# A mixture-of-experts decoder layer: slots as a list of 8-byte pairs, rows gathered by GpSimd, routing and experts in one block

## What is computed

```python
y   = attn @ Wo + bo + x1                  # x1: output of the mixer
x2  = layernorm(y)
logits = x2 @ Wr + br                      # 8 experts
top2   = top_k(logits, 2);  w = softmax(of the two)
out = layernorm(x2 + sum_i w_i * (relu(x2 @ W1[e_i] + b1[e_i]) @ W2[e_i] + b2[e_i]))
```

## Time and profile before

| | us |
|---|---|
| median of three runs | 2315.91 (2313.05 to 2318.25) |
| the profiled execution | 2310.07 |
| its span, first to last instruction | 2308.3 |
| mixer and attention, until the routing block's first instruction | 1592.4 |
| routing block until the experts' first matmul | 165.5 |
| 71 expert tiles | 514.5 |
| final norm and stores | 34 |

### The profile page before, as it was taken

One profiled execution on the slowest core, in us unless ns is written; L12 is line 12 of the kernel. 1 busy time (PEld: TensorE's weight loads), 2 busy tenths in 40 slices (PEclk: granted clock), 3 DMA queues, 4 the chain that ended last, 5 costly groups with the idle time before them and its releaser, 6 DMA issues. The chain is left out here.

```text
span 2308.3 us, 41136 instructions
## 1 busy us (share of the span) xinstructions
PE 2011.2 (87%) x10638; PEld 1052.4 (46%) x10638; DVE 1736.3 (75%) x2834; ACT 1548.3 (67%) x4346; POOL 706.3 (31%) x919
## 2 busy tenths in 40 slices
PE   6988988499999999999999998886645999999993
PEld 2454555223222232222322221112545999999993
DVE  3978784399999999999999998985663555555554
ACT  3555565399999999999999999995211333333334
POOL 0001110044444344443444341111672333333331
PEclk9989999699999999999999999998767999999997
DMA  4111104646667576675765755644732222222224
GB/s 148 41 41 69 55 32 140 126 98 100 124 117 121 127 108 119 112 124 129 108 117 113 123 112 73 88 54 140 254 141 65 37 37 37 37 37 37 37 37 155
DMA packets 130110, 217.29 MB, mean 94 GB/s; under 512 B 20290, under 2 KB 100802, under 8 KB 129938
## 3 DMA queue, kind: packets, MB, share of 16 engines
q1 hardware_dynamic: 103072, 152.25, 35.6%
q0 software_dynamic: 25440, 63.46, 9.9%
q10 hardware_dynamic: 1554, 1.05, 0.2%
HBM read 137.97 MB, written 78.72 MB: 94 GB/s over the span
## 5 line engine op out<-in xcount | busy, mean ns | idle before, releaser
L1349 ACT ACTIVATE probs<-psum,neg_max 128x512 f32<-128x512 f32 (+1 forms) x1664 | 1110.8, 773 | 64.6 <-DVE neg_max L1257 63.1
L1257 DVE TENSOR_REDUCE neg_max<-psum 128x2 f32<-128x1024 f32 (+1 forms) x832 | 986.2, 1215 | 67.7 <-PE psum L1194 59.6
L1194 PE MATMUL psum<-qst,kst 96*128 96x512 bf16 (+1 forms) x1664 | 542.1, 394 | 111.6 <-ACT probs L1349 73.7
L1349 ACT ACTIVATION_READ_ACCUMULATOR probs<-psum,neg_max 128x1 f32 (+1 forms) x1664 | 488.7, 294 | 0.0
L1194 PEld LDWEIGHTS psum<-qst,kst 96*128 96x128 bf16 (+1 forms) x1664 | 130.5, 98 | 716.7 <-ACT probs L1349 655.3
L1162 PE MATMUL psum<-probs,v_scaled 128*32 128x512 f32 (+1 forms) x3328 | 454.6, 620 | 0.0
L1845 ACT ACTIVATE hid<-psum,b 128x128 f32<-128x128 f32 x568 | 162.0, 368 | 392.6 <-PE psum L1818 392.6
L1321 POOL TENSOR_TENSOR v_scaled<-vst,inv 128x64 f32<-128x64 f32 (+1 forms) x416 | 120.9, 291 | 707.0 <-DVE inv L1226 704.8
L1879 POOL DMA_INDIRECT sums_all<-y_out,dest x71 | 154.3, 2173 | 380.3 <-DVE y_out L1924 374.5
L1818 PE MATMUL psum<-xst,w 128*128 128x128 f32 x2272 | 266.6, 276 | 0.0
L1818 PEld LDWEIGHTS psum<-xst,w 128*128 128x128 f32 x2272 | 260.7, 193 | 0.1
(11 more groups left out here) (222 smaller groups left out, 2092.7 us busy)
## 6 DMA issues: line engine op xcount, KB each, us to landing
kst<-k_parts SPq DMA_DIRECT2D x384, 112.0 KB, 6.5
k_parts<-k_out POOLq DMA_DIRECT2D x52, 336.0 KB, 3.0
w_all<-in_W SPq DMA_DIRECT2D x16, 1024.0 KB
ct<-in_ctxT SPq DMA_DIRECT2D x16, 896.0 KB, 4.7
vst<-v_all SPq DMA_DIRECT2D x64, 224.0 KB, 9.2
qst<-q_parts SPq DMA_DIRECT2D x192, 64.0 KB, 5.9
v_all<-v_out POOLq DMA_DIRECT2D x13, 896.0 KB, 4.3
rows_in<-xs SPq DMA_DIRECT2D x71, 129.0 KB, 2.0
```

Source lines behind the costliest of these rows:

```text
L1194: last = pe.matmul(psum[0:r, 2 * sbuf + i, :], kst[:, h, j, t * P:t * P + r], qst[:, h, j, :], start=True, stop=True)
L1257: v.tensor_reduce(neg_max[0:r, sbuf], psum[0:r, 2 * sbuf:2 * sbuf + 2], AX_X, ALU.min) \
L1349: act.activation(probs[0:r, pb, j, :], psum[0:r, 2 * sbuf + i, :], ACT.Exp, bias=neg_max[0:r, sbuf, i:i + 1], scale=-1.0, accum_out=sums[0 ...
```

## The change

The rows of `x2` are no longer written to the slots. `list_all` holds for each slot 8 bytes: the token number and the weight. Pads are in it from the start: one DMA copies `no_pairs` (271 KB) over the whole list in the attention block, and another zeroes 128 pad rows of `x2_rows`. In the routing, `x2` is stored twice by SP, to `sums_all` and to `x2_rows`, and GpSimd writes 64 indirect DMAs of 128 pairs to the list. In the experts, SP loads 128 pairs of a tile three tiles ahead (`load_list`), VectorE casts the token numbers to `dest` (`name_rows`), and GpSimd gathers the rows of `x2_rows` with an indirect DMA two tiles ahead (`gather`). There are no pads to write at the end.

Routing and experts stand in one block. The routing is written out for 8 sequences instead of looped, and is three deep: in step c the sequence c is normed, c - 1 gets its experts, c - 2 its slots. The normed rows are now written by ScalarE (with a bias and a scale) instead of VectorE, and GpSimd's `residual` is replaced by a third matmul with one row of ones. The first two sequences' attention output and `x1`, `xwo` and W2 of expert 0 are loaded in the attention block. Buffers of the mixer and of the attention lie in the places of `w2_all` and of one shared `area`; W2 is laid out by the host as the chip holds it.

```diff
@@ attention block, SP
                     load_context(FIRST_UNITS)
+                    sp.dma_start(list_all, a["no_pairs"]).then_inc(list_cleared, 16)
+                    sp.dma_start(x2_rows[TOKENS:TOKENS + P], a["no_rows"]).then_inc(list_cleared, 16)
+                    for e in range(W2_EARLY):
+                        load_w2(sp, e)
...
                     for b in range(B - 2, B):
                         two_rounds(b, False)
                         load_weights(b)
+                        if b == B - 2:
+                            for h in range(2):
+                                sp.wait_ge(attn_stored[h], 16 * GH * 2 * (B - 1) + OPEN)
+                                load_route(sp, h)
+                            sp.dma_start(xwo, a["xWo"].rearrange("(c p) d -> p c d", p=P)).then_inc(xwo_loaded, 16)
@@ routing and experts, SP
+                    def route_step(c):
+                        h = c % 2
+                        if c < B and c + 2 < B:
+                            sp.wait_ge(y2_ready, c + 1)
+                            load_route(sp, c + 2)
+                        if c < B:
+                            sp.wait_ge(x2_ready, c + 1)
+                            for rows_to in (sums_all, x2_rows):
+                                sp.dma_start(rows_to[c * L:(c + 1) * L]..., x2[:, h]).then_inc(x2_stored[h], 16)
+                        for e in W2_IN_STEP.get(c, ()):      # {3: (1,), 4: (2,), 5: (3,), 6: (4, 5), 7: (6, 7)}
+                            load_w2(sp, e)
-                        sp.dma_start(rows_in[:, h], xs[bass.ds(row, P)]).then_inc(rows_loaded[h], 16)
+                        sp.dma_start(list_in[:, d], list_all[bass.ds(row, P)]).then_inc(list_loaded[d], 16)
+                    def tile_step(n, it, d, left):
+                        if left >= 3:
+                            sp.wait_ge(y_scaled, n + 1 + OPEN)
+                            load_list(bass.ds(n + 3, 1), (d + 3) % DESTS)
+                    sp.wait_ge(plan, ROWS_PLANNED)
+                    sp.wait_ge(scattered, 16 * 2 * TT * B)
+                    for j in range(3):
+                        load_list(slice(j, j + 1), j)
@@ GpSimd
+                    def scatter(e):
+                        pool.wait_ge(slots_ready, e + 1)
+                        for i in range(2):
+                            for t in range(TT):
+                                at = i * TT + t
+                                pool.indirect_dma_start(
+                                    list_all, bass.IndirectOffsetOnAxis(slot_u[:, e, at:at + 1], 0),
+                                    pairs[:, e, i, t, :], None).then_inc(scattered, 16)
+                    def gather(count, d):
+                        wait_alone(pool, (dest_ready, count))
+                        pool.indirect_dma_start(rows_in[:, d % 2], None, x2_rows,
+                                                bass.IndirectOffsetOnAxis(dest[:, d, :], 0)) \
+                            .then_inc(rows_loaded[d % 2], 16)
+                    def tile_step(n, it, d, left):
+                        h = d % 2
+                        if left >= 2:
+                            wait_alone(pool, (xs_t_ready, n + 1))
+                            gather(n + 3, (d + 2) % DESTS)
                         wait_alone(pool, (y_scaled, n + 2 + OPEN), (y_added[1 - h], ...))
                         pool.indirect_dma_start(sums_all, ..., y_out[:, h], None, compute_op=ALU.add)
@@ TensorE
+                            last = pe.matmul(at, ones[0:1, :], rows[0:1, XBO, :], start=False, stop=True)
+                    def route_step(c):
+                        if 0 <= c - 2 < B:
+                            ranks(c - 2)
+                        if 0 <= c - 1 < B:
+                            turn(c - 1)
+                        if c + 1 < B:
+                            project(c + 1, (0, 1))
+                        if 0 <= c - 1 < B:
+                            route(c - 1)
+                        if c + 1 < B:
+                            project(c + 1, (2, 3))
@@ VectorE
+                    def route_step(c):
+                        if c < B:
+                            norm_rows(c)
+                        if 0 <= c - 2 < B:
+                            slots(c - 2)
+                        if c < B:
+                            shift_rows(c)
+                        if 0 <= c - 1 < B:
+                            choose(c - 1)
+                    def name_rows(d, count):
+                        v.wait_ge(list_loaded[d], count)
+                        v.tensor_copy(dest[:, d], list_in[:, d, 0:1]).then_inc(dest_ready, 1)
+                    def tile_step(n, it, d, left):
+                        h = d % 2
+                        if left >= 2:
+                            v.wait_ge(y_added[h], 16 * loads_of(it, d - 2, h))
+                            name_rows((d + 2) % DESTS, 16 * (it + (d + 2) // DESTS + 1))
@@ ScalarE
-                                last = act.activation(rows_out[:, h, i, :, 0:D], x2[:, h], ACT.Copy)
+                            for t in range(TT):
+                                last = act.activation(x2[:, h, t], y2[:, t], ACT.Identity, bias=shift2[:, t:t + 1],
+                                                      scale=rstd2[:, t:t + 1])
```

More of the change, by code:

```diff
@@ L1799, in _, with project @@
                 @block.tensor
                 def _(pe):
-                    def turn(half, count):
+                    def project(b, ts):
+                        h = b % 2
+                        if ts[0] == 0:
+                            wait(pe, y2_ready, b - 1)
+                            pe.wait_ge(route_loaded[h], 32 * (b // 2 + 1))
+                        for t in ts:
+                            at = psum[:, 2 * h + t // 2, (t % 2) * D:(t % 2 + 1) * D]
+                            for k in range(C):
+                                pe.matmul(at, at_in[:, h, k, t * P:(t + 1) * P], xwo[:, k, :], start=k == 0, stop=False)
+                            last = pe.matmul(at, ones[0:1, :], rows[0:1, XBO, :], start=False, stop=True)
+                        if ts[-1] == TT - 1:
+                            last.then_inc(proj_ready, 1)
@@ new lines, in turn, with route @@
+                    def turn(e):
+                        wait(pe, x2t_copied, e)
+                        pe.wait_ge(x2_ready, e + 1)
+                        for k in range(C):
+                            for t in range(TT):
+                                last = pe.transpose(psum[:, 4 + k, t * P:(t + 1) * P],
+                                                    x2[:, e % 2, t, k * P:(k + 1) * P], ident[:])
+                        last.then_inc(x2t_ready, 1)
+                    def route(e):
+                        wait(pe, logits_ready, e)
+                        pe.wait_ge(x2t_copied, e + 1)
+                        for t in range(TT):
+                            for k in range(C):
+                                last = pe.matmul(psum[:, 6, t * E:(t + 1) * E], x2t[:, k, t * P:(t + 1) * P],
+                                                 router_w[:, k, :], start=k == 0, stop=k == C - 1)
+                        last.then_inc(logits_z_ready, 1)
@@ L1803, in turn, with take @@
+                    def take(half, count):
                         pe.wait_ge(rows_loaded[half], count)
@@ L1832, in _ @@
                     opened(pe, mm1_done, mm2_done)
-                    turn(0, 16)
+                    pe.wait_ge(xwo_loaded, 16)
+                    project(0, range(TT))
+                    for c in range(B + 2):
+                        route_step(c)
+                    pe.wait_ge(slots_ready, B)
+                    take(0, 16)
                     tiles(pe, tile_step)
@@ L1846, in tile_step @@
                                            ACT.Relu, bias=b1[:, h, c:c + 1]).then_inc(h_ready, 1)
+                    act.preload_act_table_set("natural_log_exp_and_others")
+                    for c in range(B + 1):
+                        route_step(c)
                     tiles(act, tile_step)
@@ L1886, in _, with wide, norm_rows @@
                 @block.vector
                 def _(v):
+                    def wide(t):
+                        return t.rearrange("p t d -> p (t d)").rearrange("p (n f) -> p n f", n=2)
+                    def norm_rows(c):
+                        h = c % 2
+                        norms = Steps(NORM_STEPS * c)
+                        wait(v, x2_ready, c)
+                        v.wait_ge(proj_ready, c + 1)
+                        v.tensor_tensor(wide(y2), psum[:, 2 * h:2 * h + 2], wide(x1_in[:, h]), ALU.add) \
+                            .then_inc(y2_ready, 1)
+                        v.wait_ge(y2_ready, c + 1)
+                        for t in range(TT):
+                            v.bn_stats(stats2[:, t], y2[:, t]).then_inc(dve_norm, 1)
+                            s = norms.next()
+                        wait_alone(v, (dve_norm, s))
+                        for t in range(TT):
```

(2 more changed lines are left out.)

669 lines of the change are left out of this document (276 added, 393 removed).

## The result

The changed kernel takes 2332.64 us (2330.48 to 2335.75, four runs) against 2314.48 us for the kernel before, run beside it: a ratio of 1.0081 (1.0063 to 1.0099), slower by 18 us. The forecast was 2281 us and faster.

The account below looks back on a forecast made before the run. TensorE bounds the 71 expert tiles, no engine the routing. Routing -39 us and tiles +5 make -34: 2310.07 becomes 2276, and the median 5.8 above gives about 2281 us, range 2268 to 2293.

Parts of the forecast that it names:

- Start: Routing's beginning: TensorE starts at 1592.6, its matmuls take 6.4 us, VectorE's y of sequence 0 comes 6.9 us earlier.
- some 9.5 us a step: TensorE's step per sequence in the routing, at the mixer's granted clock of 0.88; 8.2 us at full clock, 13.5 at low.
- Rival D: Routing stays paced upstream: TensorE at the low clock, 13.5 us a step, 23 of 39 us lost, 2304 us; chance 0.13.
- To the first scatter: Routing from VectorE's y of sequence 0 to GpSimd's first scatter: 22.9 us against 18.7 before, +4.2, at 1621.9.
- Scatters: Routing's 64 indirect DMAs at 1.27 us make 81.6 us against 106.7 before; GpSimd sets the pace at 10.2 us per sequence.
- I keep 0.97: Issue of one routing scatter of 128 descriptors stays 0.97 us with 8-byte elements; bounds 0.6 and 1.06.
- 3 us for loads that come late: Allowance added to the routing's scatter time because DMA demand comes close to the limit; bounds 0 and 10 us.
- 346 GB/s would be all of it: DMA limit in the routing, from 204 GB/s at a share of 0.59; the new steps need 308 GB/s.
- To the first matmul: From the last scatter's issue at 1705.2 to the experts' first W1 matmul at 1718.7, without pads or block end.
- Expert tiles: In the 71 tiles the gather is due as it lands, at 7.35 us against 7.25: +5 us, bounds 0 and 62.
- rival B: Expert tiles: VectorE's weight copies block the gather, which lands 0.35 to 0.95 us late; 12 to 34 us, chance 0.15.
- The early loads: DMAs added ahead of the routing run beside attention and cost nothing; if that failed, some 5 us.

Follow-up runs that it names:

- W2 last: The changed kernel, matmuls of one row and gather two tiles ahead kept, with W2 of experts 1 to 7 loaded behind the last stores of x2: 2337.68 us.
- W2 behind the lists: The changed kernel with the bias matmul over 128 rows and W2 of experts 1 to 7 loaded behind the first three list loads: 2300.13 us.
- three repairs: The changed kernel with the bias matmul over 128 rows, W2 of experts 1 to 7 behind the last x2 stores, gather three tiles ahead: 2272.74 us.

## Why the prediction was wrong, step by step

**Start.** "with 4 bias matmuls of the same width 5.08 x 20/16 = 6.4 us": it measured 12.6. Two errors: a float32 matmul is two instructions, so it is 24/16, which gives 7.6 us, and the clock. Over 128 rows the first projection takes 7.1 to 7.6 us, partly at the low clock, and the next one, at full clock, 5.3.

**The clock: the step that failed.** I wrote "the new steps have short gaps, so I take the mixer's, some 9.5 us a step", explaining the 0.69 of the earlier trace rows by TensorE standing still between groups. There was not one gap, and the clock stood at 0.53 from 1600 to 1700 us; a step took 15.5 or 18.5 us in turn, 17.3 in the mean. The 8.2 us that I had for a step at full clock are what the kernels with full rows and without stops show (8.24 from logits to logits). What I had not looked at is the new instruction's shape: one row in place of 128 cost 1.05 us for every four projection instructions beside it (2.08 against 1.03). The Trainium skill, page "TensorE: Matmul & The Clock Gate", section "Part 1: The HAM clock gate", has the clock follow how busy TensorE is; the trace disagrees for this case, since TensorE was busy all the time from 1600 to 1700 us at 0.53 of the full clock, and only the contraction changed that. Rival D named the low clock, and its sign, GpSimd idle and VectorE waiting for TensorE, is the one that came; but it priced a step at 13.5 us, by the same wrong count, gave standing still as the reason, and had 0.13.

**To the first scatter.** 29.3 forecast, 27.3 to 27.8 with the clock repaired, 48.8 with it low: 21 us of the miss are the clock's.

**Scatters.** "I keep 0.97" and the pace of GpSimd were right in themselves: 80.3 to 80.6 us where nothing upstream fails. In the changed kernel it is 120.9. The runs have all four cases: 80.3 with full rows and no stop, 115.5 with one row and no stop (W2 last), 108.8 with full rows and three stops, and 120.9 with one row and one stop. So of the 41 us the low clock alone makes 35 and the stop some 5. The full rows alone gained only 12 because three stops came up in the changed kernel's order of W2 loads, where one row had one; the "3 us for loads that come late" did not hold them. Both causes have to go before GpSimd sets the pace. The "346 GB/s would be all of it" held nowhere: W2 loads alone moved 425 GB/s, and beside the scatters 253.

**To the first matmul.** 13.5 forecast, 13.3 measured.

**Expert tiles.** +5 forecast, +7.5 measured. The mechanism was right, "the gather is due as it lands", and three tiles ahead removed 6.2 of it. The mis-sized term is the gather's issue, 1.57 us beside the weight copies, where I had taken 0.97 + 0.36 = 1.33. One tile in time:

```profile
1921.79 0.38 PE L1661 MATMUL psum<-ident,rows_in 128*128 128x128 f32 x2
...
1925.35 1.21 DVE L1898 COPY area<-w_all 128x2048 f32 x1
...
1925.81 1.61 POOL L1572 DMA_INDIRECT rows_in<-x_rows,dest  x1 [0.30 <-issue]
...
1929.27 0.44 PE L1661 MATMUL psum<-ident,rows_in 128*128 128x128 f32 x2
```

The issue overlaps the second copy for 0.75 us and is 0.62 us longer than away from it: nearer to rival B's block than to my 0.36, but the tile takes 7.48 us, under the 7.6 that B starts from. (My own terms add up to 7.31 and, for the upper bound, 8.95, not to 7.35 and 8.98; neither changes anything.)

**The early loads** cost under 1 us: from the attention's first load of `qst` to the first projection it is 1197.2 us (392.83 to 1590.03), and to the forecast's 1592.6 it was 1196.6 before. The start is early because the mixer ended 3.2 us earlier in this execution, which is luck. Sum: the routing lost 57 us against the forecast and the tiles 2.5; with a start 2.6 us earlier, -34 became +22 between the two profiled executions.

**Open.** What holds up TensorE's signal in a stop. For nine of the eleven stops the trace has the update of the semaphore for which VectorE waits. It comes 6.4 to 14.9 us behind the recorded end of TensorE's logits, and VectorE goes on 0.02 us later; in the steps without a stop the update comes within 0.02 us of that end. In the stop shown above the logits end at 1634.88 and the update is at 1649.70; the update of the next projection, recorded until 1637.57, is at 1649.83. In the three kernels with more than one stop some updates of TensorE's turns and countings come up to 5.4 us late too. So VectorE is not what stood still of itself. The ends of matmuls are modelled, so whether TensorE's work was late or only its signals isn't settled. Of the causes, a delayed instruction fetch, as the expectations have it for VectorE, would have to be one that holds TensorE; in two cases a packet of an instruction queue lands within 2.5 us behind the stop, but fetches also appear in the middle of running scatters with no stop, and no run separates them. The Trainium skill, page "Runtime: NRT & Kernel Launch", section "Instruction fetch mechanics", calls the crossing of a code page mostly hidden; if the stops were fetches, they would be cases in which it isn't. Not settled either: why scatters in flight bring a stop in some kernels and in others (W2 last, W2 behind the lists, the kernel before) never do.

## What to carry to other kernels

A bias by a matmul of one row of ones looks like the cheapest work on TensorE, and here it was the dearest: ask what it does to the clock of its neighbours, and try the same sum over all rows. When a change takes one engine's waits away, price the next engine's step from its own instructions at both clock levels and put the decision there; a price per item that is right tells nothing if the engine doesn't get to pay it. Two causes can hide each other: W2 behind the stores gave nothing by itself (2337.7 us), the full contraction 27 us, both together 51 us (2281.3), and with the gather three tiles ahead 60 us. And when a wait has no releaser, compare the time of the semaphore's update with the end of the instruction that raises it before you blame the engine that waits.

## What the hardware showed that I had not expected

- One-row matmuls in the mix: granted clock 0.53 with TensorE busy 100 of 100 us in the changed kernel, 0.50 with it busy 129 of 142 us in the kernel before; 4 projection instructions in 2.08 us; full rows in their place: 0.82 (from 1600 to 1700 us) and 1.03 us.
- TensorE's semaphore updates 6.4 to 14.9 us behind the recorded end of its matmuls, in nine places, all while GpSimd's scatters were in flight; none in the two kernels whose scatters came after the steps.
- GpSimd's gather issue of 128 rows: 1566 ns beside VectorE's weight copies, 986 ns away from them.
- W2 loads beside the scatters of 8-byte pairs moved 253 GB/s at a full DMA share (three repairs), against 425 GB/s alone (128 rows, W2 behind the lists); in two windows of 10 us, first beside the scatters:

```profile
1684.00:1694.00 10.00, 0.00 (x0) 0.00 (x0) 0.80 (x3) 0.00 (x0) 7.56 (x9) 0.50 1.08 253
```

```profile
1710.00:1720.00 10.00, 0.00 (x0) 0.00 (x0) 0.00 (x0) 0.00 (x0) 0.00 (x0) 0.50 1.01 425
```
